# Four homes for normalised columns, and offsets right behind their own projection, in the value projection of a deformable convolution

## The chip, the cores and the metric

The kernel runs on one core of one Trainium2 chip, as one launch. The metric is the device time of one execution in microseconds; the time before is the median of three runs. Engines are named as in the profile: PE (matrix multiply, with PEld for its weight loads), DVE (vector), ACT (scalar), POOL (GpSimd), SP (which here only issues DMAs).

## The reference, cut to what matters

The input is two images of 128 channels by 128 by 128 pixels, in float32. Two layers follow each other, each on a group-normalised input and added to it: a window attention, and a deformable convolution. Only the second one is touched by the change:

```
def _gn(v, G=32, eps=1e-05):            # per image, 32 groups of 4 channels
    ...
    return ((g - m) / jnp.sqrt(s + eps)).reshape(v.shape)
x = x + _L0_conv_ref(_gn(x), ...)       # attention in 16 x 16 windows
x = x + _L1_conv_ref(_gn(x), ...)       # deformable convolution
# within _L1_conv_ref, per pixel (L = H*W) of xt = normalised x:
v  = xt @ value_proj_w.T + value_proj_b     # 128 values
om = xt @ offset_mask_w.T + offset_mask_b   # 8 groups x 9 taps x (dx, dy, mask)
...                                     # bilinear samples of v at pixel + tap + (dx, dy)
out = jnp.einsum('nhwkgc,nhwkg->nhwgc', sampled, mask_t)
out = out.reshape(N, L, C) @ output_proj_w.T + output_proj_b
```

So every pixel needs two projections of the same normalised column of x: its values and its offsets with their masks.

## The kernel before, in words

`attention` runs first, for both images. Then `deformable` runs the two images one after the other (loop over b). In each image there are four stages, one behind the other:

1. The attention's projection is added to x, which stays in SBUF as `x1` (128 channels by 16384 pixels), and statistics for the normalisation are taken (to L160).
2. **The value projection** (`each_step`, which calls `value(v, slot, turn)` on every engine, for v from 0 to 31). A step handles 4 image columns, 512 pixels. Steps 0 to 7 and 24 to 31 are written out; steps 8 to 23 are a loop whose body has four steps, so that there v is not a Python integer and the parts under `isinstance(v, int)` fall away.
3. The deformable groups (`each_group`, 32 groups of 4 columns): products of sampled values with tap weights on DVE (`prod`, L1581), their sums by transposing matmuls on PE (L1330), and the offsets of later groups in between.
4. The image is stored.

In a step of stage 2:

- The columns are normalised into `xn` (the trace calls it d_xn), which has two halves: ACT writes half 0 for even v (L1464), POOL writes half 1 for odd v (`normalise`, L1127). Both wait until step v-2 is projected (`v_done`), and for v from 2 to 8 also until the offsets of column v-2 have been computed (`om_done`), since these read the same half.
- PE projects them into `sum_ps` (four float32 matmuls, shown as eight, L1375). `sum_ps` has two halves as well: PE waits until DVE has read step v-2 (`vrow_ready`).
- DVE adds the bias into `vrow` (L1621; four slots, laid into the tile vring, so the trace says vring), after waiting that the store of step v-4 has landed (`vrow_out`). SP stores the slot to `vals` in DRAM (L1016, 256 KB).
- In the written-out steps other work is woven in, in the order of each engine's code. For v from 1 to 7, PE computes the offsets of column **v-1** behind the projection of v (`offsets`, L1290 and L1293, into `om_ps`, which has one buffer: PE waits until ACT has read the column before, `off_ready`). For v from 2 to 7, ACT reads the offsets of column **v-2** out of PSUM and takes their absolute size (`read_offsets`, L1419 and L1423) behind its normalisation of v. For v from 3 to 7, DVE looks for far offsets in column **v-3** (`find_far`, L1516, L1518, L1521) ahead of its bias addition; column 5 is done at v = 24. `flags` (L1532 to L1541) follows at v = 6. ACT's size of column q waits until `find_far` of column q-1 is done (`det_step`).
- Steps 24 to 31 prepare stage 3: ACT computes `hats` of group 0 (v = 24 to 26) and of group 1 (v = 29 to 31), DVE `tap_terms` of group 0 behind step 27 (L1560, L1565), PE `weights(0, 0)` behind step 30. `hats` of group 1 wait for `tap_terms` of group 0.

Behind the last store, SP loads the columns for the first products, and stage 3 begins. Every engine works through its own instructions in order; a wait holds everything queued behind it on that engine.

The counters start at one, so `wait_ge(v_done, count(b * GROUPS + v))`, with one more added at the start, holds until step v-2 has been projected.

Of the kernel before, what the change touches and what calls it, by code (L numbers as in the profile page):

```python
# [6 lines left out]
ACT = mybir.ActivationFunctionType  # L7
# [40 lines left out]
OM = 3 * K2 * G  # L48
# [26 lines left out]
PAIR = C + CG  # L75
VROWS = 4
V_FIRST, V_LAST = 8, 24
AHEAD_OFF = LEAD + 1
# [650 lines left out]
def deformable(nc, x, attended, w_proj, bproj_row, w_value, bv_row, w_om, bom_row, w_out, b_out, vals, off_out, info_out, far_sums, out):  # L729
# [3 lines left out]
    with ExitStack() as ctx:  # L733
# [60 lines left out]
        fsum = sb("fsum", [P, RING_F, COLS, C])  # L794

        scratch = prod[:, 1].rearrange("p t c -> p (t c)")[:, 0:KE].bitcast(I32)
        row_at = sb("row_at", [P, 1])
# [266 lines left out]
        def _(pool):  # L1064
# [40 lines left out]
            with pool.Fori(0, B) as b:  # L1105
# [14 lines left out]
                def normalise(v):  # L1120

                    pool.wait_ge(v_done, count(b * GROUPS + v))
                    pool.sem_inc(pool_passed, 1)
                    if 2 <= v < AHEAD_OFF + 2:
                        pool.wait_ge(om_done, count(b * GROUPS + v - 1))
                        pool.sem_inc(pool_passed, 1)
                    nc.gpsimd.tensor_scalar(xn[:, 1], cols[:, v * COLS:(v + 1) * COLS, :], gn[:, 0:1], gn[:, 1:2],  # L1127
                                            ALU.mult, ALU.add).then_inc(vn_ready[1], 1)
# [133 lines left out]
        def _(pe):  # L1262
# [9 lines left out]
            with pe.Fori(0, B) as b:  # L1272
# [10 lines left out]
                nc.tensor.matmul(a_ps[:, 0:2], gmat[:], ex[:], start=True, stop=True).then_inc(g_sum, 1)  # L1283
                def offsets(q, par):
                    n = b * GROUPS + q
                    if not isinstance(q, int) or q >= AHEAD_OFF:
                        pe.wait_ge(xn_ready, count(b * (GROUPS - AHEAD_OFF) + q - AHEAD_OFF + 1))
                    pe.wait_ge(off_ready, count(n))
                    for half in range(HALVES):
                        nc.tensor.matmul(om_ps[:, half, 0:2 * OM].rearrange("p (r o) -> p r o", r=2), bom_ones[:],  # L1290
                                         bom_rows[:].unsqueeze(1).to_broadcast([P, 2, OM]), start=True, stop=False)
                        for r in range(2):
                            mm = nc.tensor.matmul(om_ps[:, half, r * OM:(r + 1) * OM], xn[:, par, 2 * half + r, :],  # L1293
                                                  wom_sb[:], start=False, stop=(r == 1))
                    mm.then_inc(om_done, 1)
# [55 lines left out]
                def group(s):  # L1351
# [12 lines left out]
                    if s.has(LEAD + 1):  # L1364
                        offsets(s.on(LEAD + 1).q, (s.place + LEAD + 1) % 2)
                    if s.has(LEAD) and (s.place + LEAD) % EPOCH == EPOCH - 1:
# [3 lines left out]
                def value(v, slot, turn):  # L1370
# [3 lines left out]
                    for r in range(COLS):  # L1374
                        mm = nc.tensor.matmul(sum_ps[:, par, r * C:(r + 1) * C], xn[:, par, r, :], wvalue_sb[:],  # L1375
                                              start=True, stop=True)
                    mm.then_inc(v_done, 1)
                    if isinstance(v, int):
                        if 0 <= v - 1 < AHEAD_OFF:
                            offsets(v - 1, (v - 1) % 2)  # L1380
                        if v == V_LAST:
                            count_far(0)
                        if v == GROUPS - 2:
                            weights(0, 0)
# [8 lines left out]
        def _(act):  # L1393
            act.wait_ge(ones_ready, count(4))
            act.sem_inc(ssum_ready, 1)
            with act.Fori(0, B) as b:
# [58 lines left out]
                def value(v, slot, turn):  # L1455
                    if slot % 2 == 0:
                        act.wait_ge(v_done, count(b * GROUPS + v))
                        if not isinstance(v, int):
                            act.wait_ge(om_done, count(b * GROUPS + AHEAD_OFF))
                        elif 2 <= v < AHEAD_OFF + 2:  # L1460
                            act.wait_ge(om_done, count(b * GROUPS + v - 1))
                        src = cols[:, v * COLS:(v + 1) * COLS, :] if isinstance(v, int) else \
                            cols[:, bass.ds(v * COLS, COLS), :]
                        nc.scalar.activation(xn[:, 0], src, ACT.Identity, bias=gn[:, 1:2],  # L1464
                                             scale=gn[:, 0:1]).then_inc(vn_ready[0], 1)
# [15 lines left out]
        def _(dve):  # L1481
# [4 lines left out]
            with dve.Fori(0, B) as b:  # L1486
# [205 lines left out]
```

## Time and profile before

| | us |
|---|---|
| median of 3 runs | 3333.71 (3331.82 to 3335.79) |
| the profiled execution's own time | 3319.04 |
| its span | 3317.4 |
| PE, DVE, ACT, POOL busy | 2731.6, 2720.6, 1827.6, 1151.6 |
| image 1: first normalised column to last bias addition | 1646.99 to 1728.02 |
| image 2: the same | 2527.01 to 2608.38 |

The profile is one execution, with times counted from the start of its span. The attention takes its first half; the value projection of the two images is two stretches of some 81 us. In the timeline, rows with several instructions ("x8") are merged, and the last bracket tells how long the engine stood idle before and what ended that. Ends of matmuls are modelled.

### The profile page before, as it was taken

The numbers are of one execution on the slowest core, as the hardware profiler recorded it, in microseconds if no ns is written. First come the engines' busy times: TensorE is split into PE (matmuls) and PEld (weight loads), VectorE is DVE, ScalarE is ACT, GpSimd is POOL, SyncE is SP. The second block draws the span as 40 slices with busy tenths as digits, with TensorE's granted clock in tenths as the row PEclk, the third lists the DMA queues.
The fourth block names the chain that finished last, engine by engine and source line by source line (L and its number), as shares of the span: only waits on it lengthen the run. The fifth ranks groups of instructions, "written<-read, shape, count | busy, mean of one in ns | idle before, by whom it ended". The sixth has DMA issues, their size and how long they took to land.

```text
span 3317.4 us, 78066 instructions
## 1 busy us (share of the span) xinstructions
PE 2731.6 (82%) x22424; PEld 2191.1 (66%) x22424; DVE 2720.6 (82%) x6553; ACT 1827.6 (55%) x3483; POOL 1151.6 (35%) x1557
## 2 busy tenths in 40 slices
PE   0599999999999999997567999898946799989986
PEld 0355555665555666564557888888845688888885
DVE  5488888888888888886557999999945799999996
ACT  0488888888888888886043444333202443344320
POOL 0333333333333333331536322146323441115550
PEclk9999999999999999999888999999978899999998
DMA  6788888888888888885653323333364533323334
GB/s 222 128 141 140 140 142 140 140 141 142 141 139 143 141 141 140 142 142 86 213 168 87 101 90 98 97 101 100 84 244 146 152 105 97 100 88 102 103 88 162
DMA packets 350627, 432.59 MB, mean 130 GB/s; under 512 B 42224, under 2 KB 275072, under 8 KB 344304
## 3 DMA queue, kind: packets, MB, share of 16 engines
q1 hardware_dynamic: 338544, 423.85, 57.5%
q0 software_dynamic: 11904, 6.44, 1.5%
q8 instruction: 101, 1.65, 0.2%
q14 instruction: 78, 0.64, 0.1%
HBM read 283.33 MB, written 147.09 MB: 130 GB/s over the span
## 4 chain that ended last, share of the span: by engine, by line
DVE 24%; issue 10%; DMA 7%; PE 5%; POOL 3%; DVEq 1%; ACT 1%; POOLq 1%; SPq 1%; ACTq 0%
DVE prod L1581 17%; DMA vring<-vals 3%; DVE tt L1565 2%; PE sum_ps L1375 2%; DVE my L1560 2%; DMA vring<-attended 1%; DVE x L1592 1%; PE sum_ps L1330 1%; ACT d_xn L1464 1%; PE sum_ps L1279 1%; PE om_ps L1293 1%; POOL gath L1155 1%; POOLq L1162 1%; DMA o_sel<-off_out,pos 1%; DMA out<-x 1%
## 5 line engine op out<-in xcount | busy, mean ns | idle before, releaser
L590 ACT ACTIVATE prob<-sbias,nmax 128x256 f32<-128x256 f32 x2048 | 904.9, 501 | 195.6 <-DVE nmax L677 193.6
L677 DVE CUSTOM_DVE_ANT_0 sbias<-s_ps,nbias 128x256 f32<-128x256 f32 x2048 | 766.5, 420 | 223.6 <-PE s_ps L482 211.2
L1581 DVE TENSOR_TENSOR prod<-vring,wt_ps 128x1920 f32<-128x1920 f32 (+3 forms) x512 | 898.4, 1812 | 17.3 <-DMA vring<-vals 11.3
L1330 PE MATMUL sum_ps<-d_ident,prod 128*128 128x128 f32 x6400 | 772.0, 278 | 81.7 <-DVE prod L1581 81.6
L1330 PEld LDWEIGHTS sum_ps<-d_ident,prod 128*128 128x128 f32 x6400 | 731.2, 144 | 130.1 <-DVE prod L1581 103.2
L495 PE MATMUL pt_ps<-a_ident,prob 128*128 128x128 f32 x4096 | 644.9, 280 | 133.5 <-ACT prob L590 130.8
L495 PEld LDWEIGHTS pt_ps<-a_ident,prob 128*128 128x128 f32 x4096 | 447.5, 140 | 277.3 <-DVE probT L686 118.4
L1430 ACT ACTIVATE hat<-off,one_col 128x576 f32<-128x576 f32 x128 | 140.6, 1099 | 701.7 <-DVE tt L1565 701.7
L482 PE MATMUL s_ps<-stack 96*128 96x256 bf16 x2048 | 396.6, 275 | 9.1 <-DMA stack<-parts_dram 9.1
L426 POOL CAST parts<-qk 128x1024 bf16<-128x1024 f32 x64 | 66.3, 1036 | 859.6 <-ACT qk L583 859.6
L686 DVE COPY probT<-pt_ps 128x512 f32<-128x512 f32 x512 | 351.5, 687 | 12.1 <-PE pt_ps L495 12.1
L1308 PE MATMUL wt_ps<-tt,d_ident 128*128 128x144 f32 x2304 | 312.1, 291 | 5.3 <-issue 5.3
L1308 PEld LDWEIGHTS wt_ps<-tt,d_ident 128*128 128x128 f32 x2304 | 307.1, 195 | 6.8 <-issue 5.4
L482 PEld LDWEIGHTS s_ps<-stack 96*128 96x128 bf16 x2048 | 175.0, 98 | 203.0 <-issue 137.2
L597 ACT COPY probT<-pt_ps 128x512 f32<-128x512 f32 x512 | 290.1, 567 | 0.0
L510 PE MATMUL o_ps<-probT,va 128*32 128x256 f32 x4096 | 274.1, 385 | 0.9 <-DVE probT L686 0.9
L1565 DVE TENSOR_TENSOR tt<-hat,my 128x864 f32<-128x864 f32 x192 | 192.3, 1056 | 15.5 <-PE wt_ps L1308 6.9
L1170 POOL COPY first_e<-first_at 128x2 f32 x16 | 2.8, 178 | 575.1 <-issue 575.1
L677 DVE DVE_READ_ACCUMULATOR2_ANT nmax<- 128x1 f32 x2048 | 169.5, 83 | 0.0
L510 PEld LDWEIGHTS o_ps<-probT,va 128*32 128x32 f32 x4096 | 107.0, 109 | 87.7 <-issue 35.9
L1279 PE MATMUL sum_ps<-wproj_sb,vring 128*128 128x128 f32 x512 | 80.2, 317 | 88.5 <-DMA vring<-attended 79.3
L429 POOL TENSOR_TENSOR rest<-qk,parts 128x1024 f32<-128x1024 f32 x64 | 137.1, 2142 | 11.8 <-POOL parts L426 11.8
(167 smaller groups left out, 3365.1 us busy)
## 6 DMA issues: line engine op xcount, KB each, us to landing
stack<-parts_dram SPq DMA_DIRECT2D x768, 128.0 KB, 7.4
vring<-vals SPq DMA_DIRECT2D x270, 320.0 KB, 3.0
parts_dram<-parts SPq DMA_DIRECT2D x64, 768.0 KB, 6.5
off_out<-off SPq DMA_DIRECT2D x64, 432.0 KB, 3.6
strips<-x SPq DMA_DIRECT2D x68, 256.0 KB, 3.5
a_stats_in<-x SPq DMA_DIRECT2D x16, 1024.0 KB, 4.9
far_sums<-nothing SPq DMA_DIRECT2D x64, 256.0 KB, 2.1
attended<-on SPq DMA_DIRECT2D x256, 64.0 KB
```

The lines of the kernel that those rows point to most:

```text
L482: mm = nc.tensor.matmul(s_ps[:, n % 2, half, :], stack[:, par, 0, h, at:at + P], stack[:, par, 1, h, w * NT:(w + 1) * NT], start=True, sto ...
L495: mm = nc.tensor.transpose(pt_ps[:, T_BANK[n % 4], kh, half * P:(half + 1) * P], prob[:, n % 4, half, kh * P:(kh + 1) * P], ident[:])
L510: mm = nc.tensor.matmul(o_ps[32 * j:32 * j + VA, t * NT:(t + 1) * NT], va[:, par, 2 * w + kh, 4 * t + j, :], probT[:, (4 * k + j) % 8, kh, ...
L590: ins = nc.scalar.activation(prob[:, n % 4, half, :], sbias[:, n % SBIAS, half, :], ACT.Exp, bias=nmax[:, n % SBIAS, half:half + 1], scale ...
L597: nc.scalar.copy(probT[:, n % 8], pt_ps[:, T_BANK[n % 4]]).then_inc(t_read_a, 1)
L677: ins = nc.vector.tensor_tensor_reduce(out=sbias[:, n % SBIAS, half, :], in0=s_ps[:, n % 2, half, :], in1=nbias[:, h, half, :], scale=1.0, ...
L686: nc.vector.tensor_copy(probT[:, n % 8], pt_ps[:, T_BANK[n % 4]]).then_inc(t_read_v, 1)
L1308: mm = nc.tensor.matmul(acc[:, :, jx:jx + KS, jy * G:(jy + KS) * G], ident[:], tt[:, jx, jy, 2 * half:2 * half + 2].rearrange("p r (a k) - ...
L1330: mm = nc.tensor.matmul(sum_ps[:, par, r * H:(r + 1) * H], prod[:, r % 2, dx, dy * C:(dy + 1) * C], ident[:], start=(r + dx + dy == 0), st ...
L1430: nc.scalar.activation(xy(hat[:, j]), xy_off(s), ACT.Abs, bias=0.0 if j == 1 else one_col[:, j // 2:j // 2 + 1]).then_inc(dist_ready, 1)
L1565: ins = nc.vector.tensor_tensor(tt[:, jx], hat[:, jx, :, 0:KG].unsqueeze(1) .to_broadcast([P, 3, COLS, KG]), my[:], ALU.mult)
L1581: nc.vector.tensor_tensor(prod[:, r % 2, first:last].rearrange("p a (t c) -> p (a t) c", c=CG), vring[:, at:at + wide].rearrange("p a (t c ...
```

## The change

The normalised columns of the value projection get a tile of their own name, `xv`, with four places in place of the two halves of `xn`. `xv` is laid over the first 2048 of the 3200 floats (per partition) of buffer 0 of `prod`, which is first written by the products of stage 3; all four places lie there. `xn` stays for the groups of stage 3. Column v goes to place v % 4. The waits move with it: a column v of 4 and more waits until step v-4 is projected, and, where v-4 is under 7, until the offsets of column v-4 are computed. Columns 0 to 3 wait for nothing but the statistics.

PE computes the offsets of column v behind the projection of v itself (v from 0 to 6), ACT reads those of v-1 (v from 1 to 6), DVE looks for far offsets in v-2 (v from 2 to 7, so that column 5 is no longer left for v = 24), and `flags` comes at v = 5. SP's code, the hats, the tap terms and the first weights stay at their steps.

```
+        xv = prod[:, 0].rearrange("p t c -> p (t c)")[:, 0:XVS * COLS * H].rearrange("p (s r y) -> p s r y", s=XVS, r=COLS)
...
                 def normalise(v):                                   # POOL, odd v
-                    pool.wait_ge(v_done, count(b * GROUPS + v))
-                    pool.sem_inc(pool_passed, 1)
-                    if 2 <= v < AHEAD_OFF + 2:
-                        pool.wait_ge(om_done, count(b * GROUPS + v - 1))
+                    if v >= XVS:
+                        pool.wait_ge(v_done, count(b * GROUPS + v - XVS + 2))
                         pool.sem_inc(pool_passed, 1)
-                    nc.gpsimd.tensor_scalar(xn[:, 1], cols[:, v * COLS:(v + 1) * COLS, :], ...
+                        if v - XVS < AHEAD_OFF:
+                            pool.wait_ge(om_done, count(b * GROUPS + v - XVS + 1))
+                            pool.sem_inc(pool_passed, 1)
+                    nc.gpsimd.tensor_scalar(xv[:, v % XVS], cols[:, v * COLS:(v + 1) * COLS, :], ...
...
                 def value(v, slot, turn):                           # PE
-                        mm = nc.tensor.matmul(sum_ps[:, par, r * C:(r + 1) * C], xn[:, par, r, :], wvalue_sb[:],
+                        mm = nc.tensor.matmul(sum_ps[:, par, r * C:(r + 1) * C], xv[:, slot, r, :], wvalue_sb[:],
                                               start=True, stop=True)
                     mm.then_inc(v_done, 1)
                     if isinstance(v, int):
-                        if 0 <= v - 1 < AHEAD_OFF:
-                            offsets(v - 1, (v - 1) % 2)
+                        if v < AHEAD_OFF:
+                            offsets(v, xv[:, slot])
...
                 def value(v, slot, turn):                           # ACT
                     if slot % 2 == 0:
-                        act.wait_ge(v_done, count(b * GROUPS + v))
-                        if not isinstance(v, int):
-                            act.wait_ge(om_done, count(b * GROUPS + AHEAD_OFF))
-                        elif 2 <= v < AHEAD_OFF + 2:
-                            act.wait_ge(om_done, count(b * GROUPS + v - 1))
+                        if not isinstance(v, int) or v >= XVS:
+                            act.wait_ge(v_done, count(b * GROUPS + v - XVS + 2))
+                            if not isinstance(v, int):
+                                act.wait_ge(om_done, count(b * GROUPS + AHEAD_OFF))
+                            elif v - XVS < AHEAD_OFF:
+                                act.wait_ge(om_done, count(b * GROUPS + v - XVS + 1))
-                        nc.scalar.activation(xn[:, 0], src, ACT.Identity, bias=gn[:, 1:2], ...
+                        nc.scalar.activation(xv[:, slot], src, ACT.Identity, bias=gn[:, 1:2], ...
                     if isinstance(v, int):
-                        if 0 <= v - 2 < LEAD:
-                            read_offsets(first_spot(v - 2))
+                        if 0 <= v - 1 < LEAD:
+                            read_offsets(first_spot(v - 1))
...
                 def value(v, slot, turn):                           # DVE
-                    if isinstance(v, int) and 0 <= v - 3 < V_FIRST - 3:
-                        find_far(first_spot(v - 3))
-                    if isinstance(v, int) and 0 <= v - V_LAST < LEAD - (V_FIRST - 3):
-                        find_far(first_spot(v - V_LAST + V_FIRST - 3))
+                    if isinstance(v, int) and 0 <= v - 2 < LEAD:
+                        find_far(first_spot(v - 2))
...
-                        if v - 3 == EPOCH - 1:
-                            flags(first_spot(v - 3))
+                        if v - 2 == EPOCH - 1:
+                            flags(first_spot(v - 2))
```

## Rows read from the trace of the kernel before

**Rows 1.** The page, part 4: the chain that ended last, by line.

```profile
DVE prod L1581 17%; DMA vring<-vals 3%; DVE tt L1565 2%; PE sum_ps L1375 2%; DVE my L1560 2%; DMA vring<-attended 1%; DVE x L1592 1%; PE sum_ps L1330 1%; ACT d_xn L1464 1%; PE sum_ps L1279 1%; PE om_ps L1293 1%; POOL gath L1155 1%; POOLq L1162 1%; DMA o_sel<-off_out,pos 1%; DMA out<-x 1%
```

**Rows 2.** Groups by line, image 1's value projection: busy us, mean ns | idle before, releasers.

```profile
L1375 PE MATMUL sum_ps<-wvalue_sb,d_xn 128*128 128x128 f32 x256 | 38.2, 306 | 28.8 <-ACT d_xn L1464 21.5 <-POOL d_xn L1127 5.0 <-DVE vring L1621 2.3
```

**Rows 3.** Windows: us; busy PE, PEld, DVE, ACT, POOL; PEclk, DMA share, GB/s.

```profile
1647.00:1654.48 7.48, 6.07 (x26) 5.54 (x26) 1.38 (x2) 1.24 (x2) 1.20 (x1) 0.60 0.19 59
1654.48:1663.40 8.92, 5.96 (x36) 5.10 (x36) 3.85 (x8) 4.86 (x5) 1.21 (x1) 1.00 0.15 45
...
1689.96:1695.53 5.57, 4.12 (x34) 3.75 (x34) 2.77 (x4) 2.55 (x2) 2.44 (x2) 1.00 0.62 188
```

**Rows 4.** Timeline, steps 2 and 3: start, us, engine, line [idle before <-releaser].

```profile
1648.37 3.78 PE L1375 MATMUL sum_ps<-wvalue_sb,d_xn 128*128 128x128 f32 x16 [4.24 <-ACT d_xn L1464]
...
1654.48 1.25 ACT L1464 ACTIVATE d_xn<-x,d_gn 128x512 f32<-128x512 f32 x1 [6.24 <-PE om_ps L1293]
...
1655.85 1.15 PE L1375 MATMUL sum_ps<-wvalue_sb,d_xn 128*128 128x128 f32 x8 [1.41 <-ACT d_xn L1464]
1656.60 1.00 ACT L1423 ACTIVATE size<-off 128x576 f32<-128x576 f32 x1
...
1656.84 0.35 PE L1290 MATMUL om_ps<-bom_rows,bom_ones 128*128 128x432 bf16 x1
...
1657.73 0.46 DVE L1516 TENSOR_TENSOR reach<-size 128x288 f32<-128x288 f32 x1
...
1657.94 0.89 PE L1293 MATMUL om_ps<-wom_sb,d_xn 128*128 128x216 f32 x4
...
1658.68 0.45 DVE L1521 SCALAR_TENSOR_TENSOR keys<-reach,keytab 128x288 f32<-128x288 f32 x1
1659.03 0.88 ACT L1419 COPY off<-om_ps 128x864 f32<-128x864 f32 x1 [1.43 <-PE om_ps L1293]
1659.04 1.21 POOL L1127 TENSOR_SCALAR d_xn<-x,d_gn 128x512 f32<-128x512 f32 x1 [10.59 <-PE om_ps L1293]
```

**Rows 5.** Timeline, the same image: flags, then step 8 and after.

```profile
1675.50 1.35 DVE L1532 MAX8 top<-keys 128x8 f32<-128x1152 f32 x1
...
1678.49 0.44 DVE L1516 TENSOR_TENSOR reach<-size 128x288 f32<-128x288 f32 x1
...
1681.66 1.25 ACT L1464 ACTIVATE d_xn<-x,d_gn 128x512 f32 x1 [0.72 <-PE om_ps L1293]
...
1685.86 2.06 PE L1375 MATMUL sum_ps<-wvalue_sb,d_xn 128*128 128x128 f32 x16 [0.70 <-ACT d_xn L1464]
1687.05 0.69 DVE L1621 TENSOR_TENSOR vring<-sum_ps,bvalue_sb 128x512 f32<-128x512 f32 x1 [1.16 <-PE sum_ps L1375]
1687.21 1.27 ACT L1464 ACTIVATE d_xn<-x,d_gn 128x512 f32 x1 [1.53 <-PE sum_ps L1375]
```

**Rows 6.** DMA issues in image 1's value projection: xcount, KB each, us to landing.

```profile
vals<-vring SPq DMA_DIRECT2D x32, 256.0 KB, 2.3
```

**Rows 7.** Timeline, steps 24 to 31 of image 1.

```profile
1703.75 1.28 ACT L1464 ACTIVATE d_xn<-x,d_gn 128x512 f32<-128x512 f32 x1 [1.37 <-PE sum_ps L1375]
...
1704.83 1.25 POOL L1127 TENSOR_SCALAR d_xn<-x,d_gn 128x512 f32<-128x512 f32 x1 [1.54 <-PE sum_ps L1375]
...
1705.27 1.13 DVE L1516 TENSOR_TENSOR reach<-size 128x288 f32<-128x288 f32 x1
...
1708.44 1.23 ACT L1464 ACTIVATE d_xn<-x,d_gn 128x512 f32<-128x512 f32 x1
...
1718.04 1.09 ACT L1430 ACTIVATE hat<-off,one_col 128x576 f32<-128x576 f32 x1 [5.77 <-DVE tt L1565]
...
1727.33 0.69 DVE L1621 TENSOR_TENSOR vring<-sum_ps,bvalue_sb 128x512 f32<-128x512 f32 x1 [3.29 <-PE sum_ps L1375]
```

**Rows 8.** Timeline, image 2: ACT's columns 2 and 24.

```profile
2534.80 1.25 ACT L1464 ACTIVATE d_xn<-x,d_gn 128x512 f32<-128x512 f32 x1 [6.54 <-PE om_ps L1293]
...
2584.09 1.28 ACT L1464 ACTIVATE d_xn<-x,d_gn 128x512 f32<-128x512 f32 x1 [1.37 <-PE sum_ps L1375]
```

More of the change, by code:

```diff
@@ L76 @@
 VROWS = 4
+XVS = 4
 V_FIRST, V_LAST = 8, 24
@@ L1120, in normalise @@
                 def normalise(v):
-                    pool.wait_ge(v_done, count(b * GROUPS + v))
-                    pool.sem_inc(pool_passed, 1)
-                    if 2 <= v < AHEAD_OFF + 2:
-                        pool.wait_ge(om_done, count(b * GROUPS + v - 1))
+                    if v >= XVS:
+                        pool.wait_ge(v_done, count(b * GROUPS + v - XVS + 2))
                         pool.sem_inc(pool_passed, 1)
-                    nc.gpsimd.tensor_scalar(xn[:, 1], cols[:, v * COLS:(v + 1) * COLS, :], gn[:, 0:1], gn[:, 1:2],
+                        if v - XVS < AHEAD_OFF:
+                            pool.wait_ge(om_done, count(b * GROUPS + v - XVS + 1))
+                            pool.sem_inc(pool_passed, 1)
+                    nc.gpsimd.tensor_scalar(xv[:, v % XVS], cols[:, v * COLS:(v + 1) * COLS, :], gn[:, 0:1], gn[:, 1:2],
                                             ALU.mult, ALU.add).then_inc(vn_ready[1], 1)
@@ L1283, in _, with offsets @@
                 nc.tensor.matmul(a_ps[:, 0:2], gmat[:], ex[:], start=True, stop=True).then_inc(g_sum, 1)
-                def offsets(q, par):
+                def offsets(q, src):
                     n = b * GROUPS + q
@@ L1292, in offsets @@
                         for r in range(2):
-                            mm = nc.tensor.matmul(om_ps[:, half, r * OM:(r + 1) * OM], xn[:, par, 2 * half + r, :],
+                            mm = nc.tensor.matmul(om_ps[:, half, r * OM:(r + 1) * OM], src[:, 2 * half + r, :],
                                                   wom_sb[:], start=False, stop=(r == 1))
@@ L1364, in group @@
                     if s.has(LEAD + 1):
-                        offsets(s.on(LEAD + 1).q, (s.place + LEAD + 1) % 2)
+                        offsets(s.on(LEAD + 1).q, xn[:, (s.place + LEAD + 1) % 2])
                     if s.has(LEAD) and (s.place + LEAD) % EPOCH == EPOCH - 1:
@@ L1456, in value @@
                     if slot % 2 == 0:
-                        act.wait_ge(v_done, count(b * GROUPS + v))
-                        if not isinstance(v, int):
-                            act.wait_ge(om_done, count(b * GROUPS + AHEAD_OFF))
-                        elif 2 <= v < AHEAD_OFF + 2:
-                            act.wait_ge(om_done, count(b * GROUPS + v - 1))
+                        if not isinstance(v, int) or v >= XVS:
[4 more added lines that the diff above has]
+                                act.wait_ge(om_done, count(b * GROUPS + v - XVS + 1))
                         src = cols[:, v * COLS:(v + 1) * COLS, :] if isinstance(v, int) else \
                             cols[:, bass.ds(v * COLS, COLS), :]
-                        nc.scalar.activation(xn[:, 0], src, ACT.Identity, bias=gn[:, 1:2],
+                        nc.scalar.activation(xv[:, slot], src, ACT.Identity, bias=gn[:, 1:2],
                                              scale=gn[:, 0:1]).then_inc(vn_ready[0], 1)
                     if isinstance(v, int):
-                        if 0 <= v - 2 < LEAD:
-                            read_offsets(first_spot(v - 2))
+                        if 0 <= v - 1 < LEAD:
+                            read_offsets(first_spot(v - 1))
                         if V_LAST <= v < V_LAST + 3:
```

## The prediction, on record before the run

> **What bounds the kernel now.** I read the page's chain first: the long terms are DVE's products and tap terms, which belong to the attention's end and to the groups; the value projection shows as two lines of 1 to 2 per cent, its matmuls and ACT's normalisation [rows 1]. Nothing else runs in these two stretches (the statistics end just before, the products need all values just behind), so what is saved there comes off the end whole. So the second view is the groups by line inside one stretch: PE projects for 38.2 us and stands idle before those matmuls for 28.8 us, nearly all of it for ACT's and POOL's normalisation [rows 2]. The third, the windows, splits the stretch: in the steps with offsets a pair of steps takes 8.92 us with PE busy for 5.96; in the loop it takes 5.57 / 2 = 2.785 with PE busy for 2.06 [rows 3]. No engine is full in either, so each is a chain of waits, and the timeline gives it.
>
> Steps 2 to 7: normalise, project, offsets, and only then the next normalisation. ACT starts column 2 at 1654.48, PE projects at 1655.85 (0.12 behind ACT's end), starts the offsets at 1656.84 and ends them at 1657.94 + 0.89 = 1658.83; POOL's column 3, released by these offsets, starts at 1659.04 [rows 4]. The loop: ACT's column 12 at 1687.21 is released by PE's projection of column 10, which began at 1685.86, and PE in turn is released by ACT [rows 5].
>
> **The change, part by part** (image 1; t is the time on the profile's clock).
>
> *Opening, up to column 2.* Columns 0 to 3 need no release, but ACT has `read_offsets(0)` queued ahead of column 2. PE starts at the granted 0.60 of this window [rows 3]: 3.78 us for projections 0 and 1 [rows 4], so 1.89 each. Projection 0 from 1648.37 ends at 1650.3; the offsets of 0 follow, the first half still at the low level, about 2.9 us, so 1653.2 (estimate). ACT then copies (0.2 to notice, 0.88), takes sizes (1.00) and normalises column 2 from 1655.3, against 1654.48 before: a loss of 0.8 us.
>
> *Steps 2 to 7.* Now a column's own offsets hold only its fourth successor, and two shorter cycles remain. Count from the end of the offsets of an even column. ACT: copy after 0.20, 0.98 to the next start, sizes 0.95 to the next start, normalise from 2.13 to 3.38 [rows 4]. PE meanwhile projects the odd column (0.99, normalised long ago), starts its offsets when the copy is out at 1.15, and ends them at 1.15 + 1.99 = 3.14. The next even column is projected at 3.38 + 0.16 = 3.54, its offsets start at 4.53 (the odd copy ran from 3.34 to 4.22) and end at 6.52. So 6.5 us per pair in place of 8.92. `find_far`, 1.40 us from 1657.73 to 1658.68 + 0.45 [rows 4], lies beside it: sizes of an even column are ready at 2.2, it ends at 3.65, and the next sizes start at 4.3. SP's stores of offsets keep their steps and are released earlier than they are reached.
>
> `flags` comes a step earlier. From MAX8 at 1675.50 to the next reach at 1678.49 it holds DVE for 3.0 us [rows 5]. With pairs of 6.5 from 1656.7 on, projection 5 ends about 1667.3, the bias addition 1668.1, flags 1671.1, `find_far(4)` 1672.5; ACT's sizes of 5 wait for it until 1673.6, and column 8 is normalised from 1673.5, 1.3 us later than without that wait. PE has offsets 6 (no offsets 7) and projection 7 until 1673.8 to do, so little more is lost. Before it was 1681.66 [rows 5]: 8.2 us gained at column 8.
>
> *Loop, steps 8 to 23.* The cycle through the normalisation goes; four columns can be ahead. What is late next is PE itself, 2.06 per pair [rows 5], and the two halves of `sum_ps`: DVE starts 1.19 after a projection starts and takes 0.69 [rows 5], and with ACT's 0.12 taken as the gap to PE that makes 2.00 for two steps. ACT's 1.27 and POOL's 1.21 per pair are hidden. I take 2.1 (bounds 2.06 and 2.4, PE alone or half of the old slack given back). Stores: 256 KB per step land in 2.3 us [rows 6], and DVE needs the slot again 4 x 1.05 - 0.69 = 3.5 us after it let it go; the DMA share of 0.62 [rows 3] becomes 0.62 x 2.785 / 2.1 = 0.82. So ACT's column 24, released by projection 20: 1673.5 + 1.4 to projection 8 + 6 pairs x 2.1 + 1.3 = 1688.8. Before: 1703.75 [rows 7]. 14.95 us gained, of which 1.5 because ACT is released two steps earlier than it was.
>
> *Steps 24 to 31.* From column 24 ACT works through hats and column 26 without a wait in sight (1708.44, 4.69 behind column 24), then the hats of group 1 wait for DVE's tap terms until 1718.04, and column 30 is queued behind them [rows 7]. The change leaves that order, so this part moves as a whole. PE is idle more briefly ahead of projection 26, and `find_far(5)`, which began at 1705.27, is gone from DVE, but the bias additions that it held were needed only at 1708.44 + 1.23 + 0.1: 0.5 us gained, bounds -0.5 and 2.
>
> *POOL against DVE.* `reach` at 1705.27 took 1.13 us while POOL's normalisation from 1704.83 ran until 1706.08 [rows 7]; undisturbed it takes 0.46 [rows 4]. POOL's columns now run at other times and will fall into `find_far` at columns 5, 7, 9 and 11. The slack above (0.65 between `find_far`'s end and the next sizes, 2.2 at the other parity) mostly covers 0.7 us; I count nothing, with 1.2 each for 4 collisions, 4.8, as the other bound. [...]
>
> **The sum.** Per image 14.95 + 0.5 = 15.4 us. Image 2 has the same stretch: columns 2 to 24 take 2584.09 - 2534.80 = 49.29 us [rows 8], against 1703.75 - 1654.48 = 49.27 in image 1. 2 x 15.4 = 31 us. Against the profiled execution's own 3319.04 that is 3288; the median of the runs, 3333.71, lies 14.7 above that execution, and I take the 31 off it: **3303 us**. Bounds of my own case: pairs of 7.1 with the loop at 2.4 and the tail at -0.5 gain 14.95 - 1.8 - 1.8 - 0.5 = 10.9 per image (3312); pairs of 6.1, a loop of 2.06 and a tail of 2 gain 18 (3298).
>
> **The rivals.**
> A. *The loop does not quicken.* Another cycle holds it at 2.785: the store, if landing rose to 4 x 1.39 - 0.69 - 0.24 = 4.6 us. For it: the DMA share would rise to 0.82. Against: 2.3 us [rows 6] is half of that. Then column 8's 8.2 and the tail's 0.5 remain: 2 x 8.7 = 17, 3316 us.
> B. [...] Each of POOL's four columns holds a DVE instruction for its whole 1.2 us, and the sizes, the normalisation and PE wait behind it. For: `reach` at 1705.27 [rows 7]. Against: the slack. 2 x (15.4 - 4.8) = 21, 3313 us. [...]
> C. *The steps with offsets stay near 8.92*, because `om_ps` has one buffer and ACT's queue puts column v behind the sizes of v-2. For: ACT is the one engine that both cycles share. Against: its work is 4.86 of 8.92 [rows 3]. Then only the loop's 22.09 - 15.3 = 6.8 remains: 2 x 7.3, 3319 us.
> D. *Slower: PE's clock.* The place is steps 2 to 23, where the profile grants 1.00 [rows 3]; at the lower of its two levels a projection takes 1.89 [rows 4], a loop pair 3.78 against 2.785 and an offset pair about 2 x 5.96 = 11.9 against 8.92. That costs 8 x 1.0 + 3 x 3.0 = 17 per image, 3368 us. It decides from the point where the level stays low in both stretches; if only the loop falls, 8.2 + 0.5 - 8.0 leaves no change, 3332 us. For it: PE has rested often, and began at 0.60. Against: the level held at 1.00 with idle gaps of 1.4 us in each step, and these get shorter.
> E. *More than forecast*: steps 24 to 31 shrink too, since with the level kept high through projections 26 and 27 the tap terms start earlier; 2 to 4 us per image more, 3296 us.
>
> **How the numbers follow.** My case 0.64, A 0.10, B 0.10, C 0.04, D in both stretches 0.03 and in the loop alone 0.04, E 0.05. What a measurement of this kernel can tell from no change is about 0.2%, 6.7 us. Faster: my case, A, B, C and E, 0.93, of which I give 0.02 to mistakes of mine that none of these names: 0.91. Same 0.05, slower 0.04. The range runs from E's edge, 3296, to just behind A, 3317; the rivals beyond it hold some 0.11, and the rest of the 0.2 is for errors in my case's bounds.
>
> **What the profile after would show.** ACT's column 24 some 42 us behind its column 0 (now 56.8); in the loop ACT and POOL released by projections but PE without idle time for them, a pair at 2.1 us; in steps 2 to 7 a pair at 6.5 us with PE waiting for ACT's normalisation once per pair; `find_far` gone from step 24; the group stage unchanged in length. It is wrong if PE still waits for columns in the loop, if the loop waits for stores, if `reach` takes 1.1 us in most steps and PE waits behind it, or if the clock falls.

## The result: 36 us faster, and the profile after

The changed kernel takes 3298.87 us (median of 4 runs, 3296.21 to 3300.64) where the kernel before took 3334.75 beside it: a ratio of 0.9892 [0.9877, 0.9908], that is 31 to 41 us less. Forecast were 31 us less, 3303 with a range of 3296 to 3317. The profiled execution took 3300.47, with a span of 3298.8.

In the chain that ended last, by line, the value projection's normalisation has almost left the list: 1% for `d_xn` and 2% for `sum_ps` before [rows 1], now 0% for its successor (the trace calls `xv` "prod", after the tile that it is laid over) and 1%.

```profile
DVE prod L1585 17%; DVE tt L1569 2%; DMA vring<-vals 2%; DMA vring<-attended 2%; DVE my L1564 2%; DVE x L1596 1%; PE sum_ps L1378 1%; PE sum_ps L1282 1%; PE sum_ps L1333 1%; POOL gath L1158 1%; POOLq L1165 1%; PE om_ps L1296 1%; DMA out<-x 1%; DVE top L1536 0%; ACT prod L1468 0%
```

The groups by line in image 1's value projection answer [rows 2]; columns are busy us, mean ns, idle before it and who ended that:

```profile
L1378 PE MATMUL sum_ps<-wvalue_sb,prod 128*128 128x128 f32 x256 | 35.3, 291 | 14.1 <-ACT prod L1468 13.8
L1623 DVE TENSOR_TENSOR vring<-sum_ps,bvalue_sb 128x512 f32<-128x512 f32 x32 | 22.1, 691 | 24.9 <-PE sum_ps L1378 23.5 <-DMA vals<-vring 1.3
```

PE's idle time before these matmuls has halved, from 28.8 to 14.1 us; the reader should note the new name in DVE's row, a wait for a store.

The windows of the opening, of a pair of steps with offsets and of two loop bodies (four steps each) answer [rows 3], with its columns (us; busy PE, PEld, DVE, ACT, POOL; PEclk, DMA share, GB/s):

```profile
1652.85:1661.95 9.10, 7.47 (x32) 6.74 (x33) 1.38 (x2) 3.03 (x3) 2.40 (x2) 0.63 0.10 31
1661.95:1668.40 6.45, 5.85 (x38) 5.15 (x37) 4.16 (x8) 4.91 (x6) 1.54 (x1) 1.00 0.27 81
1686.55:1690.61 4.06, 3.99 (x35) 3.72 (x34) 2.77 (x4) 2.58 (x3) 2.47 (x3) 1.00 0.96 283
1690.61:1694.51 3.90, 3.83 (x33) 3.56 (x32) 2.77 (x4) 2.58 (x3) 2.31 (x3) 1.00 0.89 260
```

The opening got longer (9.10 in place of 7.48), the pair shorter (6.45 in place of 8.92), and in the loop PE is busy for 3.99 of 4.06 us: it is full. But so, nearly, are the DMA engines, at 0.96.

The timeline of steps 2 to 8 (start, us, engine, work, idle time before it and what ended that) shows the two cycles in place of the one of [rows 4]:

```profile
1661.95 1.27 ACT L1468 ACTIVATE prod<-x,d_gn 128x512 f32<-128x512 f32 x1
1663.20 1.54 POOL L1130 TENSOR_SCALAR prod<-x,d_gn 128x512 f32<-128x512 f32 x1 [7.76 <-PE om_ps L1296]
1663.35 1.15 PE L1378 MATMUL sum_ps<-wvalue_sb,prod 128*128 128x128 f32 x8 [0.36 <-ACT prod L1468]
...
1666.52 0.88 ACT L1422 COPY off<-om_ps 128x864 f32<-128x864 f32 x1 [1.32 <-PE om_ps L1296]
1667.52 0.98 ACT L1426 ACTIVATE size<-off 128x576 f32<-128x576 f32 x1
1668.40 1.28 ACT L1468 ACTIVATE prod<-x,d_gn 128x512 f32<-128x512 f32 x1
1669.66 1.42 POOL L1130 TENSOR_SCALAR prod<-x,d_gn 128x512 f32<-128x512 f32 x1 [4.93 <-PE om_ps L1296]
1669.81 1.15 PE L1378 MATMUL sum_ps<-wvalue_sb,prod 128*128 128x128 f32 x8 [0.35 <-ACT prod L1468]
...
1676.32 1.08 DVE L1545 TENSOR_SCALAR far_at<-at,row_at 128x8 int32<-128x8 f32 x1
1677.31 0.45 DVE L1520 TENSOR_TENSOR reach<-size 128x288 f32<-128x288 f32 x1
1678.74 1.01 ACT L1426 ACTIVATE size<-off 128x576 f32<-128x576 f32 x1 [1.75 <-DVE keys L1525]
1679.65 2.44 ACT L1468 ACTIVATE prod<-x,d_gn 128x512 f32 x2
1680.35 1.89 POOL L1130 TENSOR_SCALAR prod<-x,d_gn 128x512 f32<-128x512 f32 x1 [2.98 <-PE sum_ps L1378]
```

ACT's columns 2 and 4 (1661.95 and 1668.40) follow on its copy and sizes with nothing to wait for, and PE's idle time ahead of projections 2 and 4 is 0.36 and 0.35 us. `flags` ends with `far_at`; the `reach` behind it lets the sizes of 5 go (1.75 us of waiting), and these let column 8 go.

The timeline of the last steps answers [rows 7]:

```profile
1694.51 1.28 ACT L1468 ACTIVATE prod<-x,d_gn 128x512 f32<-128x512 f32 x1 [0.57 <-PE sum_ps L1378]
...
1708.18 1.07 ACT L1433 ACTIVATE hat<-off,one_col 128x576 f32<-128x576 f32 x1 [5.19 <-DVE tt L1569]
1710.00 1.25 ACT L1468 ACTIVATE prod<-x,d_gn 128x512 f32<-128x512 f32 x1
1711.38 2.07 PE L1378 MATMUL sum_ps<-wvalue_sb,prod 128*128 128x128 f32 x8 [6.21 <-ACT prod L1468]
```

Columns 24 (first row) and 30 (third) lie 15.49 us apart, before 16.13 (1703.75 to 1719.88), and the last bias addition and the first product stand behind column 24 at nearly their old distances (table below); ACT still waits 5.19 us for DVE's tap terms with column 30 queued behind.

The same marks in us behind ACT's column 0, image 1 / image 2, from the trace of each kernel (DVE's last bias addition by its start):

| kernel | column 2 | column 8 | column 24 | last bias addition | first product |
|---|---|---|---|---|---|
| before | 7.49/7.79 | 34.67/34.99 | 56.76/57.08 | 80.34/80.68 | 86.60/86.83 |
| before, again | 7.06/8.04 | 35.76/35.22 | 57.82/57.30 | 81.78/80.82 | 88.25/87.16 |
| after | 9.10/9.17 | 26.80/26.87 | 41.66/42.05 | 64.37/64.95 | 70.49/71.49 |
| after, again | 8.82/9.16 | 26.54/26.85 | 42.47/41.72 | 66.19/64.78 | 72.54/70.91 |
| e1: order alone | 9.13/9.17 | 26.83/26.86 | 48.94/48.98 | 73.83/73.92 | 79.90/80.08 |
| e2: homes alone | 1.17/1.17 | 28.35/27.85 | 44.31/45.02 | 68.59/68.45 | 74.71/74.79 |
| e3: column 30 ahead | 8.15/8.84 | 25.85/26.51 | 41.87/41.62 | 62.24/60.39 | 68.71/67.03 |
| e4: last steps | 8.53/9.16 | 26.21/26.88 | 41.51/42.23 | 58.27/58.64 | 67.99/68.73 |
| e6: loads early | 9.01/8.98 | 26.74/26.72 | 46.11/43.75 | 58.82/56.48 | 68.76/65.88 |
| e7: parts put together | 7.83/8.33 | 25.53/26.02 | 41.79/41.85 | 59.92/59.69 | 67.22/66.73 |
| e8: sizes last | 7.18/8.03 | 26.16/27.02 | 42.97/45.54 | 65.92/68.38 | 72.21/74.77 |

To the first product the two profiles of before average 87.21 us per image, the two of after 71.36: 15.85 saved per image, 31.7 in all.

### The profile page after: what moved, and what is told of

Read it like the earlier page. It is cut to its first block, busy times and chain, and to the rows that moved or that the text cites. A ratio compares the mean times of both kernels' runs of the same rounds, so it can differ in the third digit from the quotient of the medians.

```text
span 3298.8 us, 78060 instructions
## 1 busy us (share of the span) xinstructions
PE 2731.8 (83%) x22424; PEld 2192.4 (66%) x22424; DVE 2721.5 (82%) x6553; ACT 1828.9 (55%) x3483; POOL 1158.9 (35%) x1557
## 4 chain that ended last, share of the span: by engine, by line
DVE 24%; issue 10%; DMA 6%; PE 5%; POOL 3%; DVEq 1%; POOLq 1%; SPq 1%; ACT 1%; ACTq 0%
DVE prod L1585 17%; DVE tt L1569 2%; DMA vring<-vals 2%; DMA vring<-attended 2%; DVE my L1564 2%; DVE x L1596 1%; PE sum_ps L1378 1%; PE sum_ps L1282 1%; PE sum_ps L1333 1%; POOL gath L1158 1%; POOLq L1165 1%; PE om_ps L1296 1%; DMA out<-x 1%; DVE top L1536 0%; ACT prod L1468 0%
```

## Experiments

**Both kernels again.** The changed kernel: 

> The changed kernel itself, beside the kernel before on one chip. My theory (two chains through the normalised columns went, 15.7 us per image by the two traces from the first normalised column to the first product) expects a ratio of 0.9905, some 31 to 32 us. The rival, that part of the 36 us measured so far comes from stages the change does not touch (or that it was luck of the runs), expects it either again at 0.989 with the untouched stages shorter in the trace, or nearer 0.993.

3299.75 us (5 runs), ratio 0.9895 [0.9878, 0.9912]. The kernel before: 

> The kernel before once more, with a profile. The one profiled execution of before took 3319 us, below every timed run of that kernel (3324.6 to 3342.0), and the stages that the change does not touch took 3144 us in it, against 3149 to 3157 in the five profiles of changed kernels. If that was luck of one execution, this profile shows the value projections at 86.6 to 86.9 us again and the other stages at 3150 to 3165. If the change shortens the other stages in some way that I have not seen, no such thing shows: they stay near 3144.

3327.93 us, span 3326.3. What the change does not touch, the span less both stretches from column 0 to the first product, is 3317.4 - 173.4 = 3144.0 us in the first profile of before, 3326.3 - 175.4 = 3150.9 in the second, 3156.8 and 3149.8 in the two of after. So it differs by 7 us between two executions of one kernel, and by 13 us over the four; the profile on which the prediction was built was a short one. The ratio came near the rival's 0.989 again, but without its sign: the untouched stages were not shorter after the change. The 4 us of the measured 36 beyond the 32 in the two stretches are inside this spread and inside the interval; I give them no cause.

**e1, the order without the homes.** Offsets follow their own projection, but two places:

```
-XVS = 4
+XVS = 2
-   xv[:, slot ...]          # in the projection, the offsets, ACT's normalisation
+   xv[:, slot % XVS ...]
```

> Only the order is changed (offsets right behind their own projection, read and searched one step earlier); the normalised columns have two homes again, both in the products' tile. Theory: steps 2 to 7 run at 6.5 us per pair as with four homes, since the even columns are held by ACT's copy and sizes and not by the home; the loop stays at 2.78 per pair. Column 24 some 49 us behind column 0, gain 8 us per image, 16 us in all, ratio 0.995. Rival (two homes hold the first steps too): pairs near 8.9, gain under 3 us per image, ratio above 0.998.

3312.64 us (6 runs), 0.994 [0.9925, 0.9955]. Window and timeline of its loop:

```profile
1686.97:1692.59 5.62, 4.68 (x33) 3.94 (x33) 2.82 (x5) 2.56 (x2) 2.47 (x2) 1.00 0.62 188
```

```profile
1689.77 1.28 ACT L1468 ACTIVATE prod<-x,d_gn 128x512 f32 x1 [1.48 <-PE sum_ps L1378]
```

Column 8 comes at 26.83, as in the full change; the loop keeps its old length, 5.62 us for two pairs against 5.57 [rows 3]. The gain to the first product is 87.21 - 79.99 = 7.2 us per image. So the four homes buy the loop, and the first steps don't need them once the order is new.

**e2, the homes without the order.** Offsets, their reading, `find_far` and `flags` go back to their old steps:

```
-   if v < AHEAD_OFF:                 +   if 0 <= v - 1 < AHEAD_OFF:
-       offsets(v, xv[:, slot])       +       offsets(v - 1, xv[:, (v - 1) % XVS])
-   read_offsets(v - 1)               +   read_offsets(v - 2)
-   find_far(v - 2), flags at v = 5   +   find_far(v - 3), flags at v = 6, find_far(5) at v = 24
```

> Only the four homes; offsets of v-1 behind the projection of v as before, read at v-2 and searched at v-3 as before. Theory: the home is what the first steps waited for, so they run at 6.5 us per pair here too, and column 2 needs no offsets read first: column 24 some 40 to 42 us behind column 0, gain 15 to 16 us per image, ratio 0.990, like both edits together. Rival (the order is needed for the first steps, as the change's words put it first): only the loop's 6.5 us per image, ratio 0.996.

3307.5 us (6 runs), 0.9924 [0.991, 0.9938]. A pair takes the same 6.47 us as in the full change, so the homes alone open that cycle as well; but the expectation that this would bring everything fell. Timeline of its steps 4 to 8, and the windows on either side of projection 8:

```profile
1665.28 1.15 PE L1378 MATMUL sum_ps<-wvalue_sb,prod 128*128 128x128 f32 x8 [0.37 <-ACT prod L1468]
1671.75 1.15 PE L1378 MATMUL sum_ps<-wvalue_sb,prod 128*128 128x128 f32 x8 [0.37 <-ACT prod L1468]
1673.55 1.35 DVE L1536 MAX8 top<-keys 128x8 f32<-128x1152 f32 x1
1678.85 0.98 ACT L1426 ACTIVATE size<-off 128x576 f32<-128x576 f32 x1 [3.04 <-DVE keys L1525]
1681.17 17.05 PE L1378 MATMUL sum_ps<-wvalue_sb,prod 128*128 128x128 f32 x124 [3.31 <-ACT prod L1468]
```

```profile
1674.94:1681.17 6.23, 2.68 (x17) 2.08 (x16) 4.32 (x10) 3.19 (x4) 2.41 (x2) 0.97 0.39 135
1681.17:1684.39 3.22, 3.22 (x15) 3.22 (x16) 0.69 (x1) 1.90 (x2) 0.00 (x0) 0.52 0.40 152
```

`flags`, a step later, now stands ahead of the `find_far` that ACT's last sizes wait for: 3.04 us there in place of 1.75, then PE rests 3.31 us and starts the loop at a granted 0.52. With `find_far(5)` back behind column 24 the gain is 87.21 - 74.75 = 12.5 us per image. With four homes, then, the new order is worth 15.85 - 12.5 = 3.4 us per image. By the stage table 1.3 of it lies ahead of column 8, where `flags` stands, 1.4 between columns 8 and 24, where the clock stood at 0.52 for 3.22 us, and 0.7 behind column 24, where `find_far(5)` is back; that these are the causes is read from the place alone, as no run took the three apart. The two parts by themselves give 7.2 + 12.5 = 19.7, more than the 15.85 together: both open the same cycle in steps 2 to 7.

**e8, sizes behind the next even column.** This tests the worked order on ACT: column v+1 is normalised between the copy and the sizes of v-1.

```
-   read_offsets(v - 1)          # copy, sizes; then column v + 1 in the next step
+   copy(v - 1); normalise(v + 1) if it is even; sizes(v - 1)
```

> The changed kernel, with ACT's queue in steps 1 to 5 reordered: column v+1 is normalised between the copy and the sizes of column v-1 in place of behind both. By my working of steps 2 to 7 the even column then comes 1 us earlier and no longer holds PE; the pair falls from 6.46 to the cycle of om_ps, 2 x 3.14 = 6.28, column 2 comes 0.95 earlier, column 8 some 0.5 to 1.5 earlier. If the pair stays at 6.46 my working is wrong in naming ACT's queue.

3300.19 us in one run. Projections 2, 4 and 6 by its timeline:

```profile
1657.94 1.05 PE L1378 MATMUL sum_ps<-wvalue_sb,prod 128*128 128x128 f32 x8
1664.26 1.05 PE L1378 MATMUL sum_ps<-wvalue_sb,prod 128*128 128x128 f32 x8
1670.51 1.05 PE L1378 MATMUL sum_ps<-wvalue_sb,prod 128*128 128x128 f32 x8
```

PE no longer waits for ACT and the pair falls from 6.46 to 6.32 and 6.25 us (6.28 was worked out). Column 8 comes at most 0.6 us earlier, since the sizes of 5 ahead of it wait 2.28 us for `find_far`, and the time shows nothing: column 8 to column 24 took 16.8 and 18.5 us (14.9 to 15.9 in the two profiles of the change), with the granted clock at 0.81 from 1676 to 1685 us and, in image 2, a wait of 2.3 us for a store. The cycle of the prediction, ACT's copy and sizes ahead of its next column, is the one that binds.

**e5, e9, e10: what holds the loop now.** The loop left alone but for its load: e5 projects 2 of its 4 pixel columns per step, e10 stores one of the four pixel columns (64 KB in place of 256), e9 does both. In e9 and e10 all of `vals` is zeroed once at the start; the rows that the loop leaves out are then not in the output.

```
-   for r in range(COLS):                    # PE
+   for r in range(COLS if isinstance(v, int) else 2):              # e5, e9
-   [[C, P], [YP * C, COLS], [1, C]]), vrow[:, slot]         # SP's store
+   [[C, P], [YP * C, w], [1, C]]), vrow[:, slot, 0:w]       # e9, e10: w = 1 in the loop
```

> What binds the loop of steps 8 to 23 next: in the loop PE projects only two of the four columns of a step (the other values are left as they stand in PSUM). PE's share of a pair of steps falls from 2.06 to 1.03 us. If PE alone bounds the loop now (2.03 per pair), the pair falls to the cycle of sum_ps and DVE, some 1.5. If the stores are as near as the traced DMA share of 0.89 to 0.96 says, it stays at 1.85 to 2.0, with DVE waiting for stores.

> Left out: in the loop of steps 8 to 23, two of the four projections of a step and three quarters of its store (64 KB in place of 256 KB); vals is filled with zeros once ahead of the first image, which lengthens the time outside the stages read here. With the projections halved alone the loop did not quicken (column 8 to column 24 in 14.7 to 15.4 us against 14.9), but PE's granted clock was 0.71 there, so stores and clock are not told apart. If the stores held that loop, it falls here to the cycle of sum_ps and DVE, a pair of steps near 1.5 us and some 11 us from column 8 to column 24; if it was PE's clock, it stays near 15.

> The same small stores and the zeros, with all four projections. If PE alone bounds the changed kernel's loop, the pair stays at 2.03 us and column 8 to column 24 at 14.9 us; if the stores, at a DMA share of 0.9, hold it too, it falls below 14.5. A mean DMA share near 0.25 in the loop shows that the stores are small.

| | whole time, one run | column 8 to column 24, image 1/2 |
|---|---|---|
| after | | 14.86/15.18 |
| after, again | | 15.93/14.87 |
| e5, half the projections | 3291.69 | 15.62/14.96 |
| e10, a quarter of the stores | 3390.27 | 15.46/14.85 |
| e9, both | 3370.32 | 12.1/12.0 |

The whole times of e9 and e10 hold the zeroing at the start and are not compared. Windows of e5's loop, two bodies and the second of them, then rows of its timeline:

```profile
1682.95:1691.07 8.12, 5.33 (x26) 4.53 (x26) 4.06 (x6) 3.81 (x4) 3.95 (x4) 0.71 0.85 262
1686.89:1691.07 4.18, 3.43 (x14) 3.21 (x15) 2.77 (x4) 1.28 (x2) 1.15 (x1) 0.50 0.75 227
```

```profile
1686.89 1.45 DVE L1623 TENSOR_TENSOR vring<-sum_ps,bvalue_sb 128x512 f32<-128x512 f32 x2 [2.21 <-DMA vals<-vring]
1687.64 5.95 PE L1378 MATMUL sum_ps<-wvalue_sb,prod 128*128 128x128 f32 x24 [2.19 <-DVE vring L1623]
1691.08 1.36 DVE L1623 TENSOR_TENSOR vring<-sum_ps,bvalue_sb 128x512 f32<-128x512 f32 x2 [0.64 <-PE sum_ps L1378]
```

Window of e10's loop, six pairs:

```profile
2641.47:2653.50 12.03, 11.82 (x97) 11.00 (x96) 8.30 (x12) 7.73 (x7) 7.06 (x6) 1.00 0.37 118
```

Window of e9's, two bodies, and who waited around it, 1765 to 1773 (us in all, times, longest):

```profile
1765.95:1772.61 6.66, 5.33 (x34) 4.16 (x34) 5.24 (x9) 5.13 (x4) 5.08 (x5) 1.00 0.44 144
```

```profile
PE sum_ps L1376 <- DVE vring L1621: 1.6, 5, 0.6
DVE vring L1621 <- PE sum_ps L1376: 1.3, 5, 0.4
```

Neither removal alone gives anything; both together shorten the stretch by 3 us.

e10 shows PE's bound: with a quarter of the stores a pair still takes 2.0 us, PE busy for 11.82 of 12.03. e5 does not show the stores' bound. In its image 1 two pairs take 1.61 and 1.57 us at a granted 1.00 (ACT's columns at 1681.34, 1682.95 and 1684.52); then DVE waits 2.21 us for a store, PE rests with it, and behind that the granted clock is 0.50 and pairs take 2.08 and 2.11. There DVE waits for PE again, and the DMA share is 0.75. So the store wait of 2.21 us and PE's clock of 0.50 took the gain. That wait is for the store of step 8, which SP issued at 1682.91, next behind the last offset store (432 KB, issued at 1682.08), and which took 4.0 us to land where those from step 12 on take 2.3 to 2.7. DVE's waits for stores in e10 (1.0 and 0.3 us) and in the change (below) stand at the same place, steps 11 to 13, whose slots the stores of steps 7 to 9 set free. That the offset store holds these up is read from the place; no run moved it alone.

In e9 the clock stays at 1.00, and pairs take 1.57 to 1.61 us but for one of 1.92, with a store wait of 0.6 on DVE. This is near the 1.5 expected without both; the 11 us from column 8 to column 24 were not reached. PE and DVE wait there for each other, which is the expected cycle through `sum_ps`. So PE holds the loop now. A bound for the stores alone was not measured; an estimate from the change's second body (260 GB/s at a share of 0.89, so 256 KB in 0.9 us at a full share) puts it at 1.8 us per pair, near PE's 2.03.

**e3, e4, e6, e7: the last steps.** Column 30 waits behind group 1's hats for DVE's tap terms, and that part did not shorten. e3 lets ACT normalise column 30 right behind column 28:

```
+   if isinstance(v, int) and v == GROUPS - 4:                      # ACT, behind column 28
+       w = v + 2
+       act.wait_ge(v_done, count(b * GROUPS + w - XVS + 2))
+       nc.scalar.activation(xv[:, w % XVS], cols[:, w * COLS:(w + 1) * COLS, :], ...)
```

> The changed kernel with one more step: ACT normalises column 30 right behind column 28, ahead of the hats of group 1, which wait for DVE's tap terms. Theory (column 30 is the late one of the last steps, behind DVE's tap terms): projection 30 follows the bias addition of 28 and comes 2.5 us earlier, last bias addition 2.5 us earlier per image, 5 us in all, ratio to before 0.988. Rival (the store of step 25, which SP issues only behind two waits for column loads, holds the bias addition of 29 and with it projection 31): under 1 us per image, ratio 0.9893.

3288.87 us (6 runs), 0.9879 [0.9857, 0.99].

```profile
1705.34 2.07 PE L1378 MATMUL sum_ps<-wvalue_sb,prod 128*128 128x128 f32 x8 [3.64 <-DVE vring L1628]
```

The wait passes from ACT's column to DVE's bias addition, which stands behind the tap terms. e4 keeps this edit and moves the tap terms too, with the first weights, behind the last bias addition and the last projection, and issues the column loads one per step:

```
-   if v == V_LAST + 3: tap_terms(0)      +   if v == GROUPS - 1: tap_terms(0)     # DVE
-   if v == GROUPS - 2: weights(0, 0)     +   if v == GROUPS - 1: weights(0, 0)    # PE
-   load_column(all four) at v = 24       +   load_column(v - V_LAST), v = 24 to 27  # SP
```

> The changed kernel with its last eight steps put in another order: ACT normalises column 30 ahead of the hats of group 1, DVE does the tap terms of group 0 behind the last bias addition, PE the first weights behind the last projection, and SP's four early column loads go one per step from 24 to 27. Theory (the last steps are a chain ACT hats - DVE tap terms - ACT column 30 - PE weights - last projection - store - load): last bias addition 9 to 10 us earlier per image, then the first product is bound by tap terms and weights, 7 to 8.5 us earlier; 15 us less than the changed kernel, ratio to the kernel before 0.986. Rival (the loads and stores of this stretch, at a DMA share near 0.9, are the bound): under 3 us per image, ratio 0.989.

3287.81 us (4 runs), 0.9855 [0.9836, 0.9874].

```profile
1707.96 0.69 DVE L1628 TENSOR_TENSOR vring<-sum_ps,bvalue_sb 128x512 f32<-128x512 f32 x1 [3.83 <-DMA vals<-vring]
```

A store is late next: it was issued 1.7 us after its own bias addition, behind a load on SP, and took 5.4 us to land. e6 is e4 with the loads at v = 4 to 7 and the offset stores 4 and 5 at v = 6 and 7, the other four two steps earlier than before:

```
-   load_column(v - V_LAST), v = 24 to 27     +   load_column(v - EPOCH), v = 4 to 7       # SP
-   store_offsets(4), (5) at v = 24, 25       +   store_offsets(v - 2) for all six
```

> The reordered last steps of before (column 30 ahead, tap terms and first weights last), and in addition SP issues the four early column loads at steps 4 to 7 and the offset stores of columns 4 and 5 at steps 6 and 7, where the DMA share is 0.15 to 0.45. Theory (in the reordered tail the loads and stores of steps 24 to 31 are the bound: DVE waited 3.8 us for a store there): the last bias addition comes near 53 us behind column 0, the first product near 61, 7 us per image less than with the loads in the tail, ratio 0.981. Rival (tap terms and weights bound it, or the early loads only move the DMA queue): the first product stays at 66 to 68, ratio 0.985.

3285.55 us (5 runs), 0.986 [0.9841, 0.9879].

```profile
1687.46 0.69 DVE L1626 TENSOR_TENSOR vring<-sum_ps,bvalue_sb 128x512 f32<-128x512 f32 x1 [2.08 <-DMA vals<-vring]
...
1717.12 4.38 PE L1309 MATMUL wt_ps<-tt,d_ident 128*128 128x144 f32 x18
1721.91 3.55 DVE L1588 TENSOR_TENSOR prod<-vring,wt_ps 128x1920 f32<-128x1920 f32 x2 [5.15 <-DMA vring<-vals]
```

The loads now press on the loop's stores (column 24 comes 2 to 4 us later), and the first weights, 4.38 us long, end at 1721.50, together with the load that the product's row names. e7 is e3 with the weights behind projection 31 and the loads at v = 2 to 5:

> The changed kernel with column 30 ahead of the hats of group 1, the first weights behind the last projection, and the four early column loads at steps 2 to 5; tap terms and offset stores stay where they were. Theory (the last steps are late by column 30, by the weights between the last two projections and by stores behind the loads): last bias addition at 57 to 58 us behind column 0 against 60 to 62 with column 30 alone, first product at 63 to 65, ratio to before 0.985 to 0.986. Rival (the tap terms, the low clock of PE or the landing of the last stores bound the first product anyway): no better than column 30 alone, 0.988.

3289.18 us (5 runs), 0.9877 [0.9861, 0.9892].

```profile
1716.37 5.62 DVE L1590 TENSOR_TENSOR prod<-vring,wt_ps 128x1920 f32<-128x1920 f32 x3 [6.61 <-DMA vring<-vals]
```

The four reach the first product 3.0 to 4.4 us per image earlier than the change, by the stage table. Their medians lie within 4 us of each other and 10 to 14 below the change's 3298.87 and 3299.75; by the ratios only e4's interval lies wholly below the change's [0.9877, 0.9908]. Each beats the kernel before by more than the change in its median, and e3 does it with one edit on one engine; among the four the runs don't choose. e3 gave what its theory expected and a little more. The theories of e4, e6 and e7 expected more than came: the first product 7 to 8.5 us earlier (3.0 measured), at 61 (67.3) and at 63 to 65 us (67.0). In all of the four the last bias addition gains more than the first product does: behind it stand its store, the load of the first columns, and the weights, which no run took apart.

## Why the prediction was right

*Opening.* Column 2 came 1.6 us later in the first profiles (9.10 against 7.49) where 0.8 was worked out: the term was mis-sized, because the offsets of 0 took 3.75 us, 1656.10 to 1659.85, at a granted 0.53 (0.63 in the window from column 0 to column 2), where 2.9 was put in; that only their first half would run at the low level was an estimate that no row showed. From column 2 to column 8 it then took 17.7 us where 18.2 was worked out, so a part of this error was made good by another; that is luck.

*Steps 2 to 7.* 6.45 and 6.46 us per pair against 6.5. e1 and e2 show the cycle opened by either part; e8 shows that it is ACT's sizes ahead of the next column that bound it.

*`flags`.* Sizes of 5 waited 1.75 us for `find_far` (1.3 worked out for column 8) as foreseen in kind, and column 8 came at 26.80 where 26.5 was expected: 7.9 us gained in place of 8.2. In e2, with `flags` one step later, the wait is 3.04 us.

*Loop.* 2.03 us per pair against 2.1, PE full, as the bound below (2.06) had it. The DMA share was mis-sized: 0.96 and 0.89 in place of 0.82. By the loop's real length the old share would be 0.62 x 2.785 / 2.03 = 0.85, near the second body's 0.89 at 260 GB/s; the first body moved 283 GB/s, more than its own four stores (4 x 256 KB in 4.06 us, 258 GB/s), and whose bytes these are I did not take apart. It cost little: in image 1's loop DVE waited for no store (the 1.3 us in its row above stand in the last steps, at 1710.03). In image 2 it waited 0.9 and 0.3 us, and 1.0 and 0.8 in image 1 of the second profile, each time at steps 11 to 13. So the prediction's sign of being wrong, a loop that waits for stores, did show, for one or two steps (timeline of DVE):

```profile
2553.19 0.69 DVE L1623 TENSOR_TENSOR vring<-sum_ps,bvalue_sb 128x512 f32<-128x512 f32 x1 [0.87 <-DMA vals<-vring]
```

Column 24 stood at 41.66 and 42.05 (41.8 forecast), 15.1 and 15.0 us earlier than before (14.95 forecast).

*Last steps.* From column 24 to the last bias addition 22.7 and 22.9 us, before 23.6: 0.8 gained against 0.5.

*The sum.* The two stretches gave 31.7 us where 31 was forecast. The whole time fell by 36; the other 4 us were in no term, and that they did not carry the time out of the range is luck.

*Collisions.* By the instructions on `reach` (ns, shortest, median, longest; first and last start), that row of `find_far` was never lengthened, and none is left behind column 24:

```profile
L1520 DVE TENSOR_TENSOR reach<-size x6: 446/458/459, 1662.2 to 1679.8; 128x288 f32<-128x288 f32 x6
```

POOL's instructions were lengthened more often than DVE's: its columns 5, 7 and 11 took 1.54, 1.42 and 1.89 us (1.21 undisturbed, [rows 4]), and no step hung on them. One collision did lie on a chain: `far_at`, ahead of the `find_far` that holds the sizes of 5 and so column 8, took 1.08 us beside POOL's column 9 (timeline of POOL):

```profile
1676.12 1.25 POOL L1130 TENSOR_SCALAR prod<-x,d_gn 128x512 f32<-128x512 f32 x1 [5.04 <-PE om_ps L1296]
```

But before, `flags` had met POOL as well, in the instruction one ahead (timeline of DVE in the kernel before):

```profile
1677.38 1.06 DVE L1540 CAST far_at<-at 128x8 int32<-128x8 f32 x1
1678.35 0.22 DVE L1541 TENSOR_SCALAR far_at<-at,row_at 128x8 int32<-128x8 f32 x1
```

So it stood in the 3.0 us that the prediction took for `flags`, and the change neither added nor removed it: counting nothing came out right, partly by that. In these rows the collision cost 0.9 us on the chain of column 8 (1.08 - 0.22, and as the two `far_at` rows change places, no more); the 1.2 us for each of four columns, the prediction's other bound, did not come. A run without POOL's columns was not tried.

*The rivals.* A fell on the time (the loop did shorten) though its reason was there in part: DVE did wait for stores at the start of the loop, up to 1.8 us per image. B and C fell by the pairs of 6.45, B but for the 0.9 us above. D fell: the granted clock was 1.00 from step 2 to the end of the loop in both images; a lower clock inside these stretches was measured in e2 (0.52 over the 3.22 us behind a rest of 3.31 us), in e5 (0.50) and in e8 (0.81). E did not come by itself, but e3 to e7 took just those 3 to 4 us per image by edits. The measured time lies between my case and E.

## What to carry to other kernels

Where a producer and a consumer hand over two buffers, find the longest cycle through the buffer, and then the next one: here four places helped until PE was full, and the gain in the two stretches came out within 1 us of the forecast, since PE's bound stood in the rows of before and since smaller errors cancelled. When the removal of one load gives nothing, ask the timeline where the gain went: in e5 it was there for two pairs and then lost to one store wait (2.21 us) and a granted clock of 0.50, and only the removal of both loads showed the next cycle. And look at the whole span less the touched stages: it moved by 7 us between executions of one kernel, against 31 to be measured.

## What was not expected of the hardware

With half the projections in the loop (e5) the granted clock fell to a mean of 0.71 over two bodies. The lighter work alone did not do it: at the same half work it was 1.00 in e5 until DVE's wait of 2.21 us, during which PE rested for 2.19, and 1.00 in e9, whose one store wait there is 0.6 us; behind e5's wait it was 0.50. A rest of 3.31 us in e2 was followed by 3.22 us at 0.52. That the rests brought the lower clock is read from these places; no run changed a rest alone. And where POOL and DVE worked at the same time, not DVE's instructions alone were longer (`far_at` 1.08 us in place of 0.22) but POOL's normalisation too, by up to 0.7 us (1.89 in place of 1.21).
